# Value rows of the graph layer's first tile made during the mixing's sums, edge counts closed two tiles early, router and shared parts in a new order

## The chip, the core and the metric

The kernel runs on one core of a Trainium2 chip. The core has a matrix engine (TensorE, PE in the profile), a vector engine (VectorE, DVE), a scalar engine (ScalarE, ACT), a general engine (GpSimd, POOL) and a queue engine for transfers (SyncE, SP). Each runs its own list of instructions in order; they wait for each other on semaphores. The metric is the device time of one execution in microseconds.

## The reference

x is 1250 rows of 512. With xn, the layer norm of x, and 40000 edges (src, dst):

```python
Q, K, V = xn @ Wq + bq, xn @ Wk + bk, xn @ Wv + bv        # graph layer: 8 heads of 32
att = exp((Q[receivers] * K[senders]).sum(-1) / sqrt(32)) # one row for each edge
out = relu(segment_sum(att / denom[receivers] * V[senders], receivers))
gnn = xn + relu(relu(out @ Wa + ba) @ Wf + bf)

q, k, v = elu(xn @ mWq.T + bq) + 1, elu(xn @ mWk.T + bk) + 1, xn @ mWv.T + bv   # 8 heads of 64
mix = (q @ (k.T @ v)) / (q @ k.sum() + 1e-6) @ Wo.T + bo

x = x + gnn + mix
h = ln(ln(x))                                             # 64 experts, two for each row
w, idx = top_k(softmax(h @ Wr @ codebook.T / 0.7), 2)
moe = sum over the two experts of w * (silu(h @ W1[e]) @ W2[e] + b2[e])
shared = (silu(h @ Ws1 + bs1) @ Ws2 + bs2) * 0.25
y = moe + shared
x = x + (ln(x) + y + silu(ln(y) @ Wf1 + bf1) @ Wf2 + bf2)
```

## The kernel before

The rows are cut into T = 10 tiles of 125 rows; all matrices are float32. Every engine has one list of instructions written out by hand; their order is the order of work. What is shared between the lists stands in three tables at the head of the file. `TURNS` gives each PSUM result (named `mix_o`, `gnn_v`, `hidden` ...) its bank, in rings: stretches with 6, 4, 6, 2 and 8 banks. Before PE fills a bank it waits (`turn`) until the result that had the bank before was read. `STEPS` says behind which results PE does the next steps of the edge counts. `BESIDE` says which parts of shared work stand beside which pair of expert blocks.

The stages, in order. (1) Norm, transposes of xn, the mixing's queries (`mix_q`), keys and values (`mix_kv`), with the sums k.T v over all tiles in two banks. (2) DVE puts the sums into `kvb` (lines 807 to 815), PE does `rb`, a small product for the router's bias (line 1476), and waits for `kvb_made`. Then come `mix_o` for ten tiles (line 1485; DVE divides, lines 824 to 830), their transposes `moT`, and the output product `mix_wo`. (3) The graph layer's queries and keys, 12 blocks `gnn_qk` (line 1507), which ACT reads (line 1232) and DVE splits in four goes into `qk_hi` and `qk_lo` (lines 846 to 848), stored by POOL to `qk_d`; then the value rows, ten tiles `gnn_v` (line 1513), to which DVE adds the bias (line 856).

Edge counts run beside stages 1 to 3. The 40000 edges are taken in GE = 80 groups. For a group, DVE makes one-hot matrices (lines 749, 751), PE multiplies them into one of two banks (line 1425), and DVE adds the result to `Cx` (line 755) at an offset. One step on DVE is: wait for the group before and add it, then make the one-hots for the group two ahead. PE's step g waits until group g-2 was added. After the last group DVE closes with `cx_made`. PE then transposes `Cx` (line 1530) into `C`, copied by ACT and DVE in turn; SP waits for `cx_made` too, and loads the split queries and keys of the heads (lines 452, 453) into room that the edges' buffers had. (4) Attention with the counts as weights; (5) the two products of the graph layer (`gnn_a`, `gnn_f`), norms, and the rows `yz`, stored to `z_d` for the experts.

(6) The router: logits, the best two of 64, `M1` and `M2` as one-hots and their sum `Mb` (`m_made`). PE sums `Mb`: bank `rank` 0 gives counts for each expert, `rank` 1 and 2 the rank of each row within its expert (line 1660). From the counts DVE makes blocks of 64 rows (`blocks_made`), PE sums these (`base`), DVE compares (`passed_made`), PE gives the blocks' owners (`owner`), after which SP may load experts' weights (`owner_made`). From ranks and base come positions, one-hots `slots` and `rowhot` (`slots_made`), and from them, by PE, the list of rows for each block (`list`), by which POOL gathers rows `Zg`. The combine weights (`wtop`, `prob`, `comb_made`, lines 995 to 1010) are made on DVE between `m_made` and `blocks_made`; PE transposes them (`combT`). Parts of the shared expert fill PE's list in between: `hidden` i (two halves of 8 matmul instructions each, line 1626, read by ACT with silu) and `fb` (line 1692), a fold of the last norm's bias into `bf1`.

(7) The loop over 36 pairs of blocks (and more, if the rows need them). In pair p PE does: the first product (line 1714), the second of pair p-1 (line 1732), the parts in `BESIDE[p]`, two transposes, and the transposes of the gathered rows of pair p+2 (line 1704). The parts are halves of `hidden` 6 to 19 and thirds of `shared` 0 to 7 (line 1640), laid out by the costs in `parts_beside`. POOL gathers (line 601), scatters results (line 606) and in pairs 2 to 11 adds a bias row to XR (line 622), in one list. (8) The experts' rows are read back, normed, and the last two products give the output.

## Time and profile before

| | us |
|---|---|
| median of 3 runs (905.36 to 906.53) | 905.95 |
| the profiled execution | 907.27 |
| its span | 905.5 |
| PE busy in it | 863.5 |
| DVE busy | 522.0 |
| ACT busy | 288.9 |
| POOL busy | 154.0 |

The profile is of one execution. In a timeline a row is a run of equal instructions; the number in brackets is how long the engine was idle before the first, and behind the arrow stands what ended that. Rows named PEld are weight loads that overlap the matmuls. The granted clock is PE's, as a share of 2.4 GHz; 0.50 is 1.2 GHz. In the table of stretches each engine has its busy time and its number of instructions.

### The profile page before, as it was taken

What the parts mean: (1) busy time and instruction counts of PE and PEld (TensorE: products, weight loads), DVE (VectorE), ACT (ScalarE), POOL (GpSimd) and SP (SyncE); (2) the same over time, 40 slices, a digit from 0 to 9 for tenths busy, and PEclk for the clock granted to TensorE, in tenths of its full rate; (3) what the DMA queues carried; (4) which work ended last, traced back from release to release, by engine and by line L of the source; (5) the groups of instructions that cost most, each with busy time, mean ns of one, the idle gap of its engine ahead of it and who ended that gap; (6) DMA issues with size and microseconds to landing.
All of it is one profiled execution on the core that took longest, in us unless ns stands there. A gap on an engine that the chain in (4) does not pass through costs nothing.

```text
span 905.5 us, 11877 instructions
## 1 busy us (share of the span) xinstructions
PE 863.5 (95%) x3978; PEld 492.8 (54%) x3978; DVE 522.0 (58%) x1365; ACT 288.9 (32%) x560; POOL 154.0 (17%) x168
## 2 busy tenths in 40 slices
PE   3999998999998999999999998999999999999898
PEld 2565556745577443344356586546645745654374
DVE  7687777666675899999955484222222223122472
ACT  4531111200104656565434431212222222322273
POOL 6100003200100000000001222234422222222240
PEclk9999998999999999999999998999999999999999
DMA  9410000000418350501022515688989888886722
GB/s 273 158 48 0 1 1 1 1 0 1 167 60 175 76 115 1 114 4 44 11 105 55 179 34 208 252 301 306 318 302 322 312 321 278 325 301 220 182 69 91
DMA packets 41340, 129.81 MB, mean 143 GB/s; under 512 B 8393, under 2 KB 8835, under 8 KB 40639
## 3 DMA queue, kind: packets, MB, share of 16 engines
q1 hardware_dynamic: 32955, 110.76, 37.9%
q0 software_dynamic: 7872, 17.94, 5.4%
q8 instruction: 33, 0.54, 0.2%
q10 hardware_dynamic: 452, 0.34, 0.2%
q14 instruction: 28, 0.23, 0.1%
HBM read 118.48 MB, written 19.68 MB: 153 GB/s over the span
## 4 chain that ended last, share of the span: by engine, by line
PE 67%; DVE 15%; DMA 5%; DVEq 5%; issue 4%; ACT 2%; POOL 1%; SPq 1%; POOLq 0%; ACTq 0%
DVE att L929 8%; PE ps L1464 8%; PE ps L1714 7%; PE ps L1640 7%; PE ps L1732 6%; PE ps L1626 5%; DMA Zg<-z_d,gat 4%; PE ps L1442 4%; PE ps L1498 4%; PE ps L1591 4%; PE ps L1507 4%; PE ps L1425 3%; PE ps L1582 2%; PE ps L1704 2%; PE ps L1783 2%
## 5 line engine op out<-in xcount | busy, mean ns | idle before, releaser
L1073 DVE TENSOR_SCALAR hgT<-ps,cols 128x128 f32<-128x128 f32 x152 | 51.8, 403 | 153.0 <-PE ps L1704 152.9
L929 DVE TENSOR_TENSOR att<-ps,C 125x832 f32<-125x832 f32 (+1 forms) x120 | 119.2, 1005 | 5.6 <-ACT ps L1245 4.9
L1245 ACT ACTIVATE ps<-ps 125x832 f32<-125x832 f32 (+1 forms) x120 | 96.4, 847 | 62.5 <-PE ps L1543 62.5
L1554 PE MATMUL ps<-att,V 125*64 125x416 f32 (+1 forms) x480 | 100.7, 530 | 1.4 <-DVE att L929 1.0
L1626 PE MATMUL ps<-hT,Ws_s 128*128 128x250 f32 x320 | 75.2, 387 | 0.4 <-issue 0.4
L1640 PE MATMUL ps<-Ws_s,hsT 128*125 128x512 f32 x160 | 75.3, 608 | 0.0
L1714 PE MATMUL ps<-W,hgT 128*64 128x256 f32 x576 | 71.6, 392 | 1.0 <-DVE hgT L1073 1.0
L1464 PE MATMUL ps<-mW,xnT 128*125 128x512 f32 x160 | 72.2, 594 | 0.0
L1626 PEld LDWEIGHTS ps<-hT,Ws_s 128*128 128x128 f32 x320 | 60.5, 194 | 20.4 <-issue 13.7
L1732 PE MATMUL ps<-W,ehT 128*64 128x512 f32 x288 | 68.0, 592 | 0.7 <-ACT ehT L1323 0.7
L1543 PE MATMUL ps<-Qst,Kst 128*125 128x416 f32 (+1 forms) x240 | 66.1, 386 | 2.2 <-DVE att L929 1.2
L606 POOL DMA_INDIRECT y_d<-eo,lst x35 | 35.6, 1018 | 181.3 <-ACT eo L1331 181.3
L751 DVE TENSOR_SCALAR ohB<-iotaW,key 125x200 bf16<-125x200 f16 x320 | 64.6, 265 | 0.0
L1543 PEld LDWEIGHTS ps<-Qst,Kst 128*125 128x125 f32 x240 | 37.8, 185 | 47.9 <-issue 30.7
L1331 ACT COPY eo<-ps 128x512 f32<-128x512 f32 x36 | 21.1, 586 | 113.5 <-PE ps L1732 113.5
L1323 ACT ACTIVATE ehT<-ps,b1T 128x64 f32<-128x64 f32 x144 | 33.5, 318 | 69.3 <-PE ps L1722 69.3
L1554 PEld LDWEIGHTS ps<-att,V 125*64 125x64 f32 x480 | 26.5, 135 | 49.9 <-DVE att L929 26.4
L1640 PEld LDWEIGHTS ps<-Ws_s,hsT 128*125 128x125 f32 x160 | 28.0, 187 | 46.3 <-issue 46.3
L1714 PEld LDWEIGHTS ps<-W,hgT 128*64 128x64 f32 x576 | 38.8, 139 | 21.7 <-DVE hgT L1073 1.2
L564 POOL DMA_DIRECT2D z_d<-yz x10 | 5.5, 549 | 249.9 <-DVE yz L964 249.8
L601 POOL DMA_INDIRECT Zg<-z_d,gat x38 | 40.0, 1052 | 39.6 <-DVEq L1090 26.8
L1425 PEld LDWEIGHTS ps<-ohB,ohA 125*128 125x128 bf16 x320 | 30.7, 114 | 27.1 <-issue 24.3
(249 smaller groups left out, 1208.3 us busy)
## 6 DMA issues: line engine op xcount, KB each, us to landing
W<-in_W SPq DMA_DIRECT2D x144, 512.0 KB, 6.3
Kst<-qk_d SPq DMA_DIRECT2D x32, 156.2 KB, 5.4
Qst<-qk_d SPq DMA_DIRECT2D x32, 156.2 KB, 5.6
Yt<-y_d SPq DMA_DIRECT2D x10, 448.0 KB
Ws_s<-in_Ws SPq DMA_DIRECT2D x2, 2048.0 KB, 9.7
qk_d<-qk_hi POOLq DMA_DIRECT2D x4, 625.0 KB, 3.4
qk_d<-qk_lo POOLq DMA_DIRECT2D x4, 625.0 KB, 4.6
z_d<-yz POOLq DMA_DIRECT2D x10, 250.0 KB, 2.7
```

The costliest lines, as they stand in the source:

```text
L751: i = V_.tensor_scalar(ohB[:, s, j, :], iotaW[:, :], key[:, bass.ds(k + j, 1)], None, ALU.is_equal)
L929: V_.tensor_tensor(att[:, n % 3, :, 0:w], scores_of(n, w), C[:, s, o:o + w].unsqueeze(1).to_broadcast([P, 2, w]), ALU.mult).then_inc(att_m ...
L1073: i = V_.tensor_scalar(hgT[:, u, k, :], bank(u, 128, 128, k * 128), col("g1", k), col("b1ln", k), ALU.mult, ALU.add)
L1245: S_.activation(b, b, ACT.Exp, scale=float(DK) ** -0.5).then_inc(s_exp, 1)
L1425: i = MM(bank(b, WN), ohA[:, s, :, j], ohB[:, s, j, :], start=j == 0, stop=j == EG - 1)
L1464: i = MM(bank(b, D, P), xnT[:, k, t * P:t * P + P], mW[:, 1 + w, k, :], start=k == 0, stop=k == KD - 1)
L1543: k = MM(scores_of(n, w)[:, j, :], Kst[:, h % 4, s * P:s * P + P], Qst[:, h % 4, o:o + w], start=True, stop=True)
L1554: k = MM(sums_of(i, 64 * j, 64, w), V[:, s, pair, j:j + 2, :], att[:, n % 3, j, 0:w], start=s == 0, stop=s == T - 1, skip_group_check=True)
L1626: j = MM(bank(b, 250, 128, 250 * half), Ws1_s[:, k, (2 * g + half) * 128:(2 * g + half + 1) * 128], hT[:, k, c * 250:c * 250 + 250], start ...
L1640: i = MM(bank(b, D, P), hsT[:, t // 2 % 2, k, (t % 2) * P:(t % 2) * P + P], Ws2_s[:, k, :], start=False, stop=k == DSH // 128 - 1)
L1714: i = MM(bank(2, DFF, 128, DFF * u)[R * j:R * j + R], hgT[:, u, k, R * j:R * j + R], W1[2 * u + j][:, k, :], start=k == 0, stop=k == KD - ...
L1732: i = MM(bank(4 + u, D)[R * j:R * j + R], ehT[:, u, m, R * j:R * j + R], W2[2 * u + j][:, m, :], start=m == 0, stop=m == 1, skip_group_che ...
```

## The change

1. `gnn_v` of tile 0 is done by PE between `rb` and the wait for `kvb_made` (the wait for the `gW` weights is moved there), and read by DVE right after `rb_s`.
2. `STEPS`: the last `gnn_qk` block gets two count steps, `gnn_v` tiles 1 to 7 one each, tiles 8 and 9 none. DVE closes the counts after tile 7 and reads tiles 8 and 9 behind `cx_made`.
3. Router, DVE: the combine weights are made behind `slots_made`; the second half of the ranks is copied behind `passed_made`. PE: the second half of the ranks stands behind `base`; `hidden` 2 to 5 between `owner` and `list`; `hidden` 6, `combT` and `hidden` 7 behind `list`. ACT reads in this order.
4. `hidden` 6 and 7 leave the loop. `fb` moves from ahead of the loop into it, behind `shared` 3; DVE folds `Wf1_s` there. The table that follows from the costs puts thirds of `shared` 0 and 1 beside pairs 0 (two), 1, 2, 3 and 4, `hidden` 8 from pair 5 on, and both halves of `fb` with half a hidden part beside pair 15. Before, pairs 0 and 1 had `hidden` 6 and 7, and pairs 2 to 6 `shared` 0 and 1.

```diff
@@ -132,7 +132,7 @@
...
-             "mix_wo": [2, 1, 2, 1, 2, 1, 2, 1, 2, 2], "gnn_qk": [1] * 12, "gnn_v": [1, 1, 1, 0, 1, 1, 1, 0, 1, 1]}
+             "mix_wo": [2, 1, 2, 1, 2, 1, 2, 1, 2, 2], "gnn_qk": [1] * 11 + [2], "gnn_v": [0] + [1] * 7 + [0] * 2}
@@ -149,12 +149,12 @@
...
-        if c == 0:
-            parts += [("hidden", i, k) for i in (6, 7) for k in range(2)]
-        else:
+        if c:
             parts += [("hidden", i, k) for i in range(first, first + 4) for k in range(2)]
         parts += [("shared", t, k) for t in (2 * c, 2 * c + 1) for k in range(3)]
-    cost = {"hidden": 4 * 250, "shared": 3 * 512}
+        if c == 1:
+            parts += [("fb", 0, k) for k in range(2)]
+    cost = {"hidden": 4 * 250, "shared": 3 * 512, "fb": 530}
     total, done, table = sum(cost[p[0]] for p in parts), 0, [[] for _ in range(PAIRS0)]
     for part in parts:
         table[min(PAIRS0 - 1, done * PAIRS0 // total)].append(part)
@@ -816,6 +816,13 @@
...
+            def v_kept(t):
+                reads("gnn_v", t)
+                V_.tensor_tensor(V[:, t, :, 0:3:2, :], bank(TURNS.bank("gnn_v", t), HEADS * DK, P).rearrange("p (h j d) -> p h j d", j=2, d=DK),
+                                 row("gbv", HEADS * DK).rearrange("p (h j d) -> p h j d", j=2, d=DK), ALU.add).then_inc(dve_read, 1)
+
+            v_kept(0)
...
-            for t in range(T):
...
+            for t in range(1, 8):
+                v_kept(t)
                 counted_before("gnn_v", t)
...
             v.drain().then_inc(cx_made, 1)
+            for t in (8, 9):
+                v_kept(t)
@@ -991,24 +998,10 @@
...
-            v.wait_ge(gap_exp, 1)
-            V_.tensor_scalar(sm[:, 2, :], sm[:, 1, :], 1.0, None, ALU.add)
...
             V_.tensor_copy(idh[:, :, :], idw[:, :, :])
...
             reads("rank", 0)
@@ -1016,9 +1009,11 @@
...
-            for i in range(2):
+            def ranks(i):
                 reads("rank", 1 + i)
                 V_.tensor_copy(rankS[:, 5 * i:5 * i + 5, :], bank(TURNS.bank("rank", 1 + i), 5 * E, P).rearrange("p (t e) -> p t e", t=5)).then_inc(dve_read, 1)
+
+            ranks(0)
             reads("base", 0)
...
             V_.scalar_tensor_tensor(mine[:, :], iotaB[:, :], starts_s[:, 0:1], passed[:, :], ALU.is_ge, ALU.subtract)
+            v.drain().then_inc(passed_made, 1)
+            ranks(1)
+            v.drain()
             V_.tensor_tensor(rankS[:, :, :], rankS[:, :, :], base_s[:, 0:E].unsqueeze(1).to_broadcast([P, T, E]), ALU.add)
-            v.drain().then_inc(passed_made, 1)
+            v.drain()
...
             v.drain().then_inc(slots_made, 1)
 
+            v.wait_ge(gap_exp, 1)
+            V_.tensor_scalar(sm[:, 2, :], sm[:, 1, :], 1.0, None, ALU.add)
+            v.drain()
+            V_.reciprocal(wtop[:, :, 0:1], sm[:, 2, :].unsqueeze(2))
+            v.drain()
...
+            V_.tensor_scalar(prob[:, :, :], prob[:, :, :], 4.0, None, ALU.mult)
+            v.drain().then_inc(comb_made, 1)
@@ -1088,18 +1102,22 @@
...
+            def fold_last():
+                reads("fb", 0)
+                V_.tensor_tensor(bf1F[:, :], bank(TURNS.bank("fb", 0), 2), col("bf1", 0, 2), ALU.add).then_inc(dve_read, 1)
+                for k in range(KD):
+                    V_.tensor_scalar(Wf1_s[:, k, :], Wf1_s[:, k, :], col("gf", k), None, ALU.mult)
+                v.drain().then_inc(f1_folded, 1)
+
...
+                    if name == "fb" and part == 1:
+                        fold_last()
                 rows_turned(p + 2, p % 2)
@@ -1305,15 +1323,14 @@
...
-            for i in range(4):
+            for i in range(7):
                 shared_hidden(i)
-                if i:
+                if 1 <= i <= 3:
...
-            for i in range(4, 6):
-                shared_hidden(i)
+            shared_hidden(7)
@@ -1475,6 +1492,16 @@
...
+            def graph_v(t):
+                b = turn("gnn_v", t)
+                for k in range(KD):
+                    i = MM(bank(b, HEADS * DK, P), xnT[:, k, t * P:t * P + P], gW[:, 2, k, :], start=k == 0, stop=k == KD - 1)
+                i.then_inc(filled, 1)
+                count_after("gnn_v", t)
+
+            pe.wait_ge(gw_in, 48)
+            graph_v(0)
 
             pe.wait_ge(kvb_made, 1)
             pe.wait_ge(qT_made, 12)
...
+            for t in range(1, T):
+                graph_v(t)
@@ -1652,18 +1674,20 @@
...
+            rank(0)
             pe.wait_ge(blocks_made, 1)
             b = turn("base", 0)
             MM(bank(b, E + 1, P), nblk[:, :], triS[:, :], start=True, stop=True)
             MM(bank(b, 1, E, E + 1), triI[:, :], nblk[:, 0:1], start=True, stop=True).then_inc(filled, 1)
-            whole_hidden(2)
+            rank(1)
...
-            whole_hidden(3)
+            for i in range(2, 6):
+                whole_hidden(i)
+            pe.wait_ge(slots_made, 1)
+            b = turn("list", 0)
+            for n in range(TOPK * T):
+                i = MM(bank(b, 3 * NP), rowhot[:, n, :], slots[:, n, :, :].rearrange("p s q -> p (s q)"), start=n == 0, stop=n == TOPK * T - 1)
+            i.then_inc(filled, 1)
+            whole_hidden(6)
             pe.wait_ge(comb_made, 1)
...
+            whole_hidden(7)
...
+            def last_bias(m):
+                if m == 0:
+                    pe.wait_ge(wf1_in, 16)
+                    turn("fb", 0)
                 for k in range(KD):
-                    i = MM(bank(b, 1, 128, m), Wf1_s[:, k, m:DFF:2], col("bfln", k), start=k == 0, stop=k == KD - 1)
-            i.then_inc(filled, 1)
-            read_by_now("combT", 2)
-            read_by_now("hidden", 5)
-            read_by_now("list", 0)
-            read_by_now("fb", 0)
+                    i = MM(bank(TURNS.bank("fb", 0), 1, 128, m), Wf1_s[:, k, m:DFF:2], col("bfln", k), start=k == 0, stop=k == KD - 1)
+                if m:
+                    i.then_inc(filled, 1)
@@ -1742,6 +1769,8 @@
                 for name, i, part in BESIDE[p]:
                     if name == "hidden":
                         shared_hidden(i, part)
+                    elif name == "fb":
+                        last_bias(part)
                     else:
                         shared_rows(i, part)
```

Not quoted: the order of the banks in `TURNS` follows the new order of work, and the steps from `wtop` to `comb_made` are moved as they are.

## Rows read from the trace of the kernel before

**Rows 1.** The page's first part: busy time, share and instructions of each engine.

```profile
PE 863.5 (95%) x3978; PEld 492.8 (54%) x3978; DVE 522.0 (58%) x1365; ACT 288.9 (32%) x560; POOL 154.0 (17%) x168
```

**Rows 2.** Timeline, wait for `kvb`, quotients: start us, us, engine, line, op, count [idle<-releaser].

```profile
154.01 14.02 PE L1485 MATMUL ps<-kvb,qT 128*125 128x130 f32 x80 [2.44 <-DVEq L815]
...
163.85 0.76 DVE L830 TENSOR_TENSOR mo<-ps,zt 125x256 f32<-125x256 f32 x2
...
168.88 0.76 DVE L830 TENSOR_TENSOR mo<-ps,zt 125x256 f32<-125x256 f32 x2
```

**Rows 3.** Timeline, first value tiles and the count that PE waits for.

```profile
250.99 1.91 PE L1513 MATMUL ps<-gW,xnT 128*125 128x256 f32 x8
...
256.09 0.35 DVE L755 TENSOR_TENSOR Cx<-Cx,ps 128x200 f32 x1
...
256.58 0.51 PE L1425 MATMUL ps<-ohB,ohA 125*128 125x200 bf16 x4 [1.58 <-DVE Cx L755]
...
257.42 0.41 DVE L856 TENSOR_TENSOR V<-ps,rows 125x256 f32<-125x256 f32 x1
```

**Rows 4.** Timeline, end of the counts to the first scores.

```profile
272.61 0.51 PE L1425 MATMUL ps<-ohB,ohA 125*128 125x200 bf16 x4
...
273.70 0.36 DVE L755 TENSOR_TENSOR Cx<-Cx,ps 128x200 f32 x1 [0.20 <-DVE Cx L755]
275.09 0.35 SPq L452 DMA_DIRECT2D Kst<-qk_d  x1
...
275.12 12.85 PE L1530 MATMUL ps<-ident,Cx 128*125 128x128 f32 x100 [2.00 <-DVEq L880]
...
289.37 1.22 PE L1543 MATMUL ps<-Qst,Kst 128*125 128x416 f32 x5 [0.25 <-DMA Qst<-qk_d]
```

**Rows 5.** Table of stretches, PE alone: stretch us, PE busy (count), PEclk, DMA, GB/s.

```profile
255.30:258.70 3.40, 2.12 (x13) 1.00 0.87 353
...
275.80:279.20 3.40, 3.40 (x19) 0.50 0.77 194
279.20:288.00 8.80, 8.77 (x80) 1.00 1.04 221
```

**Rows 6.** Timeline, the router up to the first pair.

```profile
526.91 0.17 DVE L995 TENSOR_SCALAR sm<-sm 125x10 f32<-125x10 f32 x1
...
531.03 0.28 DVE L1013 TENSOR_SCALAR blkI<-ps 64x125 int32<-64x125 f32 x1
...
532.01 0.31 PE L1664 MATMUL ps<-triS,nblk 64*125 64x65 bf16 x1 [1.07 <-DVEq L1018]
...
532.39 5.01 PE L1626 MATMUL ps<-hT,Ws_s 128*128 128x250 f32 x16
...
538.14 0.25 DVE L1041 TENSOR_SCALAR owner<-ps 1x104 int32<-1x104 f32 x1 [1.41 <-PE ps L1672]
...
542.58 3.54 PE L1626 MATMUL ps<-hT,Ws_s 128*128 128x250 f32 x16
...
548.45 2.44 PE L1685 MATMUL ps<-slots,rowhot 125*128 125x156 bf16 x20 [2.32 <-DVEq L1063]
...
554.89 1.93 PE L1692 MATMUL ps<-cols,Wf_s 128*128 128x1 f32 x16
...
559.46 3.44 PE L1714 MATMUL ps<-W,hgT 128*64 128x256 f32 x16 [0.98 <-DVE hgT L1073]
```

**Rows 7.** Timeline of light pairs, and the table of waits from 556 to 842 us.

```profile
599.47 1.05 POOL L601 DMA_INDIRECT Zg<-z_d,gat  x1 [0.16 <-issue]
...
606.70 0.75 PE L1704 MATMUL ps<-ident,Zg 128*128 128x128 f32 x4 [0.88 <-DMA Zg<-z_d,gat]
...
607.38 1.95 PE L1714 MATMUL ps<-W,hgT 128*64 128x256 f32 x16
614.46 1.95 PE L1714 MATMUL ps<-W,hgT 128*64 128x256 f32 x16
...
PE ps L1704 <- DMA Zg<-z_d,gat: 2.6, 6, 0.9
```

64 lines of the change are left out of this document (19 added, 45 removed).

## The prediction, made before the change was timed

> **What bounds the kernel now.** I read the page first: TensorE (PE) is busy for 863.5 of 905.5 us [rows 1], so a gain can come from three things only: its waits, its half clock, and work that is put where it waited. So I went on with the timeline of PE around its long waits, and looked for what the change touches there. The reader should see three places. (a) At 154.01 PE had been idle for 2.44 us, until VectorE (DVE) had built `kvb` [rows 2]. (b) Between the queries' rows and the attention it waits twice: 1.58 us at 256.58 for DVE to add a count [rows 3], and 2.00 us at 275.12 for `cx_made`; the SyncE (SP) loads of heads, which wait for the same semaphore, start at 275.09, and the second score waits at 289.37 for the landing of one of them [rows 4]. (c) In the router it waits 1.07 us for `blocks_made` and 2.32 us for `slots_made` [rows 6]; then comes the pair loop, where PE hardly waits: 2.6 us in six waits, all for a gathered row tile `Zg` [rows 7]. Last the clock: its granted rate falls to 0.50 after the longer waits and comes back to 1.00 some 3.4 us later [rows 5]. After the waits of 2.44, 2.00 and 2.32 us it fell; after that of 1.58 us it did not [rows 3, 5].
>
> All sums are made on the profiled execution, 907.27 us with a span of 905.5; the median of the runs is 905.95, 1.3 less. I take the saving in us from the one and subtract it from the other.
>
> **Part A, value rows of tile 0 before the `kvb` wait.** Eight matmul instructions, 1.74 us of PE (1.91 with the last one's drain [rows 3]), go into the 2.44 us wait; the `gW` weights were loaded long before (the wait for them is moved along, and 110 us lie between). PE does them in time that was lost, and 0.7 us of waiting is left. DVE gets one addition of 0.42 us (as its fellow at 257.42 [rows 3]) between `rb_s` and the first division; the first quotient had to wait for PE anyhow. What is gained in this stage is the clock. With the wait it was half for two stretches (6.8 us), and the ten tiles of `mix_o` took until 169.64 (168.88 plus 0.76 [rows 2]). At full clock DVE sets the pace, 1.258 us a tile ((168.88 - 163.85) / 4 [rows 2]). The first tile would end some 2.0 us after 154.01, at 156.0, and nine more at 167.3: **-2.4 us**. What excludes more: DVE's pace. If the remaining 0.7 us, with the nearly empty one-column matmuls of `rb` ahead of it, still drops the clock, the stage gains nothing and pays up to 0.2 us for the addition. Ends: -2.6 to +0.2. I take -2.4, since a rest of 0.7 us is nearer to the 1.58 us that did no harm.
>
> **Part B, counts closed two tiles early.** In this stretch PE loses tile 0 (1.74 us, done in A). One count step moves ahead, after the last query/key block. For DVE that is one more step (add, one hot A, one hot B: 1.33 us from 256.09 to 257.42 [rows 3]) ahead of the fourth split into `qk_hi` and `qk_lo`; all behind it on DVE is late by some 1.2 us: the split, the two POOL stores of it (which nobody wants before `cx_made`), the router's weights, the fill of `V`, and the first count that PE waits for. PE by contrast gets to that count later only by its own steps: it does block 11, two counts, tile 1, a count, tile 2, and is there at 255.2; the add that lets it on ends at 257.75 instead of 256.5. So the wait of 1.58 us becomes some 2.55 us. From there 7 tiles and 6 counts are left (7 x 1.74 + 6 x 0.345 = 14.25 us) and PE ends at 272.0 instead of 272.96.
> The last count is now two tiles (3.5 us) before that, at 268.5. In the trace 1.39 us pass from the start of the last add to the first load of the heads (273.70 to 275.09 [rows 4]), so `cx_made` comes at about 270.0 and PE, with work until 272.0, no longer waits for it. For its own branch on `levels` I put 0.3 us (0 to 0.9, the time DVE's same branch takes in that 1.39). The 100 transposes then run at full clock: 19 of them went in the 3.4 us at half clock, about 80 in 8.8 us at full [rows 5], so 1.5 us less, 11.35 in place of 12.85. PE is through at 283.65 instead of 287.97 and copies take 0.7. The loads of the heads start 5.05 us earlier, and the one that ended last lands at 284.3. Both releases meet at 284.4 against 289.37 [rows 4]: -4.9 us. The additions for tiles 8 and 9 (2 x 0.42) come on DVE behind `cx_made` and before its first copy of `C`; PE's ring waits for that of tile 8 only with the third transposed block.
> Against it: the longer wait of 2.55 us is of the length after which the clock fell each time. A half-clock stretch inside PE's own chain costs half its 3.4 us, 1.6 to 1.7, and delays the last count too. I take it as happening, since 2.55 is nearer to 2.00-2.44 than to 1.58: **-3.3 us**, ends -4.9 and -1.7 (a second half-clock stretch in the transposes).
>
> A rule of the Trainium skill speaks against the clock's share here. Rows first: PE did nothing but transposes from 279.2 to 288.0 and the granted clock was 1.00 [rows 5]. The Trainium skill, "TensorE: Matmul & The Clock Gate" (Part 4: PE-mode transpose), says that transposes do not count as busy and do not bring the full clock. By that rule a stage of 100 transposes would stay at or fall to half clock, 17.9 us at the pace of 19 in 3.4 us, and part B would lose 1.5 to 6.5 us of its gain. The row disagrees with it, and my sum goes by the row; I give the rule 0.01, inside rival 1.
>
> **Part C, the router.** On DVE the combine weights (526.91 to 531.03, 4.1 us less 0.5 for three id instructions that stay [rows 6]) go behind `slots_made`. On PE the second half of the ranks is done after `base`, hidden parts 2 to 5 stand between `owner` and `list`, 6 and 7 follow, and the bias fold `fb` goes into pair 15 of the loop. Step by step, in the trace's time: `m_made` 526.83; block counts 527.6; first ranks until 528.5 (15 of the 55 matmuls that took 3.4 us); `blocks_made` at 528.6, since DVE is now free, so the 1.07 us wait is nearly gone; `base` until 529.05; 40 ranks until 531.5; DVE has `passed_made` at 530.5; `owner` until 532.25. Four hidden parts at 3.54 to 3.57 us [rows 6], plus 1.4 for a half clock after the ranks as now (5.01 against 3.54 [rows 6]): 547.95. DVE: ranks, sums and the owner block give `owner_made` near 535.7 and `slots_made` at 544.8 (owner row at 534.6; in the trace 10.3 us lie between that row at 538.14 and `list` at 548.45 [rows 6]), 3.1 us ahead of PE, so the 2.32 us wait is gone, and with it the half clock in `list` (2.44 to about 1.4). `list` ends at 549.4, hidden 6 and 7 with the transposed weights (1.23) between them at 557.8; `comb_made` (548.8) is long there. The gathers start 1.5 us earlier than now and land under hidden 6. Transposes 1.2 and the 0.98 us wait for `hgT` [rows 6]: first pair at 560.0, **+0.5 us** against 559.46. But the loop has two hidden parts less (7.14) and `fb` more (1.79 of the 1.93 with drain [rows 6]): **-5.35 us**; and without the waits and one-column matmuls ahead of it the first pair runs at full clock (1.88 in place of 3.44 [rows 6]): **-1.55 us**.
> What can eat this is the gather. It goes out at 599.47, behind that pair's scatter and an addition of POOL, and PE waits for it at 606.70: 7.2 us [rows 7]. A pair with one third of shared rows lasts 7.08 us (607.38 to 614.46 [rows 7]). POOL sends the gather of pair p+3 about 7.1 us after pair p starts (while it still has an addition in each pair) and PE wants it 0.6 us before pair p+2 starts: two pairs must last 7.1 + 7.2 + 0.6 = 14.9 us, two light ones last 14.2. In the new table of parts the light pairs come right at the start: one third each in pairs 1 to 4, then a half hidden part alone (6.15 us) in pairs 6, 9, 16, 19, 26 and 29, against 8, 17 and 26 before. Walking the pairs with these numbers I get waits of 0.8, 0.9 and 0.8 us up to pair 10, and some 4.1 in all against 2.6: **+1.5 us**, ends 0 and +5 (every light pair pays 0.7). Sum of C: 0.5 - 5.35 - 1.55 + 1.5 = **-4.9 us**, ends -6.4 and -1.4. The fold in pair 15, 1.8 us of one-column matmuls, could drop the clock once, 1.7 us; I leave it for the range. DVE's own share of the fold (1.3 us) lies in waits of about 5 us per pair.
>
> **Sum.** -2.4 - 3.3 - 4.9 = -10.6 us: 896.7 for the profiled execution, **895.4** against the median.
>
> **Rivals.**
> 1. *The clock doesn't come back* (the waits that remain drop it all the same). A gives 0, B's transposes stay part slow (-1.8), C loses the 1.0 in `list` and the 1.55 in the first pair (-2.3). For it: where a full wait went, thin matmuls remain (`rb`, ranks, `fb`). Against it: 1.00 after a wait of 1.58 us [rows 5]. Together -4.1: 901.8.
> 2. *The gathers bind the loop.* PE work taken out of the first pairs turns into waiting for `Zg`; C gives only what comes ahead of the loop, about -1. For it: the 14.9 against 14.2 us above. Against it: 2.6 us of such waits in 36 pairs [rows 7], though there were 13 or more light ones. -2.4 - 3.3 - 1 = -6.7: 899.3.
> 3. *Slower.* Late gathers feed on themselves: if a gather in the light pairs needs more than 8.5 us to land (7.2 seen [rows 7]), each of the 20 or so light pairs waits 1 us; if a wait passes 2 us the clock falls too, 1.7 us a time. From +12 us in the loop on (1.5 counted and 10.6), the gain of all else is gone; 20 pairs at 1.0 us, less the 1.5 already counted, make 895.4 + 18.5 = 913.9. Half of the light pairs existed before and did not do so.
> 4. *The stretch isn't early.* If PE's branch on `levels`, or the DVE step ahead of the split, costs as much as the two tiles cover, B gives nothing: -7.3, 898.7.
> 5. *Better than the sum:* no half clock after the 2.55 us wait, no more gather waits than now: -13.7, 892.3.
>
> **Chances.** Forecast, within 2.5 us of 895.4: 0.48. Rival 1: 0.16. Rival 2: 0.12. Rival 4: 0.08. Rival 5: 0.07. Rival 3: 0.05, and 0.04 that several of 1, 2 and 4 come together and leave nothing that can be told from 905.95. A measurement of this kernel tells about 0.2% (1.8 us) from no change. So faster 0.91, same 0.04, slower 0.05. The range 891.5 to 902.0 takes in the forecast and rivals 1, 2, 4 and 5.
>
> **What would show it.** A: PE's wait at `mix_o` 0.7 instead of 2.44 us, and granted clock near 1 there; the ten tiles of quotients done 13.3 instead of 15.6 us after `kvb`. B: an idle time of PE of 2.5 us at the first count behind tile 2, a half-clock stretch after it; none before the transposes; last release of the scores still a head's load or a copy of `C`, within 0.5 us of each other. C: no PE wait before `base` and `list` over 0.3 us, first pair at full clock, waits for `Zg` of 3 to 5 us in all. The prediction is wrong if the `Zg` waits pass 7 us, if the clock is half in `mix_o`, or if the heads' loads, not the transposes, start the attention by more than a microsecond.

## The result, and the profile after

| | before | after |
|---|---|---|
| median, six runs each, same chip | 906.24 (904.48 to 908.81) | 897.24 (896.39 to 898.97) |
| ratio, with its 95% interval | | 0.9904 (0.9887 to 0.9922) |
| the profiled execution, its span | 907.27, 905.5 | 896.39, 894.6 |

The change makes the kernel 8.7 us faster (7.1 to 10.2). The forecast was 895.4, the range 891.5 to 902.0; the measured 897.24 lies 1.8 us above the forecast. Executions of one kernel differ by 2 to 10 us (the 31 runs of the kernel before beside the last experiments went from 903.59 to 910.1), so a profiled execution is one draw from such a spread. What is read off a trace below is set against a median wherever a kernel was run for it.

The page of the kernel after, its first part (busy time, share, instructions of each engine), which answers to [rows 1]:

```profile
PE 858.5 (96%) x3978; PEld 488.3 (55%) x3978; DVE 523.0 (58%) x1365; ACT 288.5 (32%) x560; POOL 153.9 (17%) x168
```

PE is busy for 5 us less (863.5 to 858.5) with the same 3978 instructions, so these 5 us are for the most part clock: the mean granted clock was 0.987 of full speed over 905.5 us and 0.992 over 894.6, which makes, as an estimate, 23.5 us at half clock before and 14.3 after, worth 4.6 us. The span is 10.9 us less, so 5.9 more are waits that went.

**Part A.** Timeline of PE and DVE around the wait for `kvb` (start us, us, engine, line, operation, count, idle time before and its releaser), against [rows 2]:

```profile
151.06 1.99 PE L1499 MATMUL ps<-gW,xnT 128*125 128x256 f32 x8
153.58 9.55 PE L1512 MATMUL ps<-kvb,qT 128*125 128x130 f32 x64 [0.53 <-DVEq L815]
...
153.69 0.41 DVE L821 TENSOR_TENSOR V<-ps,rows 125x256 f32<-125x256 f32 x1
...
166.81 0.75 DVE L837 TENSOR_TENSOR mo<-ps,zt 125x256 f32<-125x256 f32 x2
```

What is left of the wait is 0.53 us, the first value tile (151.06) stands where PE was idle, and from the end of the wait to the end of the last quotient 13.98 us pass (166.81 + 0.75 - 153.58) instead of 15.63. The kernel before had its half clock here from 152.9 us on, for 6.8 us; the kernel after has none.

**Part B.** Timeline from the count that PE waits for to the second score, against [rows 3, 4]:

```profile
255.30 0.35 DVE L755 TENSOR_TENSOR Cx<-Cx,ps 128x200 f32 x1
...
255.80 0.51 PE L1442 MATMUL ps<-ohB,ohA 125*128 125x200 bf16 x4 [2.52 <-DVE Cx L755]
...
268.76 0.35 SPq L452 DMA_DIRECT2D Kst<-qk_d  x1
...
270.10 11.08 PE L1552 MATMUL ps<-ident,Cx 128*125 128x128 f32 x100
...
281.90 0.43 PE L1565 MATMUL ps<-Qst,Kst 128*125 128x416 f32 x1 [0.72 <-DVE C L893]
282.80 1.20 PE L1565 MATMUL ps<-Qst,Kst 128*125 128x416 f32 x5 [0.47 <-DMA Qst<-qk_d]
```

The wait at the count has grown to 2.52 us, as forecast (2.55). The wait ahead of the transposes is gone, the loads of the heads start 6.33 us earlier (275.09 to 268.76) and the second score 6.57 us (289.37 to 282.80). The table of stretches of the kernel after, PE alone (stretch, us and PE busy with count, granted clock, DMA share, GB/s), against [rows 5]:

```profile
252.00:255.80 3.80, 1.28 (x6) 1.00 0.41 163
255.80:259.20 3.40, 3.40 (x21) 1.00 0.47 194
270.10:281.20 11.10, 11.08 (x101) 1.00 1.02 222
285.20:288.60 3.40, 3.35 (x10) 0.50 1.05 220
513.90:517.30 3.40, 3.00 (x9) 0.50 0.28 113
```

No half clock follows the wait of 2.52 us. The transposes run at full clock through 11.1 us. But two half-clock stretches stand where the kernel before had none: behind the first scores, and in the first hidden parts of the router.

**Part C.** Timeline of PE in the router, and of the fold in pair 15, against [rows 6]:

```profile
524.51 0.24 PE L1688 MATMUL ps<-triS,nblk 64*125 64x65 bf16 x1
528.26 15.06 PE L1648 MATMUL ps<-hT,Ws_s 128*128 128x250 f32 x64
543.16 1.53 PE L1703 MATMUL ps<-slots,rowhot 125*128 125x156 bf16 x20
554.49 1.95 PE L1741 MATMUL ps<-W,hgT 128*64 128x256 f32 x16 [0.98 <-DVE hgT L1087]
...
671.88 2.04 PE L1722 MATMUL ps<-cols,Wf_s 128*128 128x1 f32 x16
```

The row for `Zg` (a tile of gathered rows) in the table of waits from 540 to 835 us (total, times, longest), against [rows 7]:

```profile
PE ps L1731 <- DMA Zg<-z_d,gat: 2.8, 4, 0.9
```

`base` and `list` are not waited for, `list` takes 1.53 us in place of 2.44 and the first pair 1.95 in place of 3.44: both at full clock. The waits for `Zg` are what they were.

From mark to mark, in the two profiled executions:

| mark | before | after | gain so far | gain of the step |
|---|---|---|---|---|
| wait for `kvb` ends | 154.01 | 153.58 | 0.43 | 0.43 |
| last quotient starts | 168.88 | 166.81 | 2.07 | 1.64 |
| second score | 289.37 | 282.80 | 6.57 | 4.50 |
| attention over (`gnn_a` starts) | 450.53 | 445.55 | 4.98 | -1.59 |
| first pair | 559.46 | 554.49 | 4.97 | -0.01 |
| last pair | 829.59 | 818.73 | 10.86 | 5.89 |

The first 0.43 us belong to no part: in the profiled kernels that have everything up to this wait as before, it ended anywhere from 152.64 to 154.04 us.

### The profile page after: what moved, and what is told of

It reads as the page before. It is cut to its first block, busy times and chain, and to the rows that moved or that the text cites. A ratio compares the mean times of both kernels' runs of the same rounds, so it can differ in the third digit from the quotient of the medians.

```text
span 894.6 us, 11880 instructions
## 1 busy us (share of the span) xinstructions
PE 858.5 (96%) x3978; PEld 488.3 (55%) x3978; DVE 523.0 (58%) x1365; ACT 288.5 (32%) x560; POOL 153.9 (17%) x168
## 4 chain that ended last, share of the span: by engine, by line
PE 68%; DVE 14%; DMA 5%; issue 4%; DVEq 4%; ACT 2%; POOL 1%; SPq 1%; POOLq 0%; ACTq 0%
DVE att L936 8%; PE ps L1481 8%; PE ps L1662 7%; PE ps L1741 7%; PE ps L1648 6%; PE ps L1759 6%; DMA Zg<-z_d,gat 4%; PE ps L1459 4%; PE ps L1525 4%; PE ps L1613 4%; PE ps L1533 4%; PE ps L1442 3%; PE ps L1604 2%; PE ps L1731 2%; PE ps L1812 2%
## 5 line engine op out<-in xcount | busy, mean ns | idle before, releaser
L755 DVE TENSOR_TENSOR Cx<-Cx,ps 128x200 f32 x80 | 28.5, 356 | 29.9 <-PE ps L1442 17.2
```

## The experiments

Each kernel was timed in five rounds beside the kernel before; a ratio is always to that one, whose median was 905.9 to 906.1 throughout. A difference to the kernel after is one of medians from different rounds; by the ratios the same differences come out up to 0.8 us smaller or larger.

### One part at a time

**A alone.** The first value tile early, the counts' places as before:

```diff
...
-             ... "gnn_qk": [1] * 12, "gnn_v": [1, 1, 1, 0, 1, 1, 1, 0, 1, 1]}
+             ... "gnn_qk": [1] * 12, "gnn_v": [0, 1, 1, 1, 1, 1, 1, 0, 1, 1]}
...
+            pe.wait_ge(gw_in, 48)
+            graph_v(0)
 
             pe.wait_ge(kvb_made, 1)
```

> Only tile 0's value rows are made ahead of the wait for kvb; the counts close after tile 9 as before, the router is as before. Theory: the stage of the quotients gains 1.65 us by the clock (as in the trace after the change, 13.98 instead of 15.63 us), and the stretch of value rows gains the whole tile, 1.74 us, because the wait at its first count keeps its 1.58 us: 3.4 us in all. Rival (the parts add up as their stages did in the changed kernel, where the tile's 1.74 us turned into a longer wait at that count, 2.52 us): 1.65 us only.

Measured 903.67, ratio 0.9976 (0.9957 to 0.9996): -2.2 us, with an interval from 0.4 to 3.9 that takes in the theory and the rival. The trace goes with the theory: the wait at the first count of the value rows is 1.59 us as before, the second score is 3.16 us earlier and the end of the attention 3.11.

**B alone.** All ten value tiles behind the queries and keys; the counts closed two tiles early:

```diff
...
-             ... "gnn_qk": [1] * 12, "gnn_v": [1, 1, 1, 0, 1, 1, 1, 0, 1, 1]}
+             ... "gnn_qk": [1] * 11 + [2], "gnn_v": [0] + [1] * 7 + [0] * 2}
...
             v.drain().then_inc(cx_made, 1)
+            for t in (8, 9):
+                v_kept(t)
```

> Only the counts close two tiles early; tile 0 stays with the other tiles, the router is as before. Theory: the wait at the late count is 0.85 us instead of 2.52, since PE has tile 0 to do in it; the second score starts 4.5 us earlier relative to the first query block, as with both parts, and the half clock either stays away from the transposes and from what follows (4.5 us gained) or falls on the start of the attention (2.9). Rival (the gain needs tile 0 moved away): 2.8 us at the second score.

Measured 902.22, ratio 0.9957 (0.994 to 0.9974): -3.9 us. B is worth something without A. In its trace the wait at the count is 1.13 us (0.85 expected), the second score is 4.18 us earlier, nearer to the theory's 4.5 than to the rival's 2.8, and no half clock stands in the transposes or behind the scores.

**C alone.** The router's new order, hidden 2 to 7 ahead of the loop, and the fold in pair 15; value rows and counts as before. PE's list of it in short:

```diff
-            whole_hidden(2)
+            rank(1)
             pe.wait_ge(passed_made, 1)
...
-            whole_hidden(3)
+            for i in range(2, 6):
+                whole_hidden(i)
+            pe.wait_ge(slots_made, 1)
...
+            whole_hidden(6)
             pe.wait_ge(comb_made, 1)
...
+            whole_hidden(7)
```

> Only the router and the shared parts are in the new order. Theory (PE's work taken out of the loop comes back in full, because the gathers wait no more than before): first pair at the same time or up to 0.5 us later, loop 5.9 us shorter: -5.5 to -6.5 us. Rival (gathers bind): the waits for Zg grow from 2.6 to over 5 us and no more than 3.5 us are gained.

Measured 901.87, ratio 0.9954 (0.9936 to 0.9971): -4.2 us. In its trace `list` starts without a wait, the first pair takes 1.95 us, and the loop from first to last pair is 265.3 us against 270.1. The rival is out: the waits for `Zg` are 2.6 us in seven. The theory's 5.5 to 6.5 us lie at the upper end of the interval (2.6 to 5.8) or above it. One loop is no exact measure either: with the table of parts of the kernel before it took 269.2 to 272.1 us in seven profiled kernels, with that of the kernel after 263.1 to 265.3 in five.

The three make 10.3 us in sum, and together 8.7 (7.1 to 10.2) were measured: within these errors they add up. The forecast's terms (2.4, 3.3, 4.9) each lie inside the interval of their kernel (0.4 to 3.9, 2.4 to 5.4, 2.6 to 5.8), so the medians cannot say which is high and which low; the traces can, below.

### Is A's gain the clock?

The kernel before with only this added, work that nobody uses, so that all it can bring is the clock:

```diff
+            pe.wait_ge(gw_in, 48)
+            b = turn("mix_o", 0)
+            for k in range(KD):
+                MM(bank(b, HEADS * DK, P), xnT[:, k, 0:P], gW[:, 2, k, :], start=k == 0, stop=k == KD - 1)
             pe.wait_ge(kvb_made, 1)
```

> The kernel before, with eight matmul instructions (four products of tile 0 with the value weights, result overwritten) put into PE's wait for kvb as pure extra work; nothing else moves. Theory (part A gains in its stage by the clock alone): no half clock in the quotients, time 1.65 to 2.1 us less although work was added. Rival (the clock falls anyway, or what helps is that work was moved): no change, 0 +- 0.5 us.

Measured 905.66, ratio 1.0 (0.9987 to 1.0014). In the trace of it the mechanism works: the wait is 0.53 us, and the quotients take 13.72 us instead of 15.63, at full clock. Yet nothing is left at the end: the interval (1.2 us faster to 1.3 slower) leaves out the theory's 1.65 to 2.1. The same kernel again:

> The same as e_dummy, a second time, to narrow its interval. The profile of the first showed the quotients 1.9 us shorter and a half-clock stretch at the start of the attention, 2.6 us longer; the times showed no gain. Theory (the clock in the quotients is worth 1.9 us on average, and the stretch in the attention was that execution's): both runs together at least 1 us under before. Rival (the gain is given back on average too): within 0.7 us of before.

Measured 905.52, ratio 0.9995 (0.9978 to 1.0011), so the two together are far from the theory's 1 us or more. The timeline of PE of the first of the two shows where the gain stops, in order of time:

```profile
272.29 11.18 PE L1534 MATMUL ps<-ident,Cx 128*125 128x128 f32 x100 [2.00 <-DVEq L880]
284.19 0.42 PE L1547 MATMUL ps<-Qst,Kst 128*125 128x416 f32 x1 [0.72 <-DVE C L886]
286.33 1.20 PE L1547 MATMUL ps<-Qst,Kst 128*125 128x416 f32 x5 [1.72 <-DMA Qst<-qk_d]
```

and its table of stretches (columns as above) has the clock behind them:

```profile
287.60:291.00 3.40, 2.22 (x6) 0.50 1.02 210
```

Here the wait of 2.00 us ahead of the transposes is not followed by a half clock. They are through in 11.18 us, and then PE waits 1.72 us for the loads; the half clock comes behind that, at the attention's start, and the attention takes 163.8 us in place of 161.2. The second score is 3.0 us earlier than before, the end of the attention 0.4.

This led to a table over the profiled executions, the main finding of the study. The half clock is read from the granted clock in tables of stretches like the one above:

| kernel | first load of the heads | second score | between | half clock in the transposes | half clock behind the scores | second score to `gnn_a` |
|---|---|---|---|---|---|---|
| before | 275.09 | 289.37 | 14.28 | yes | no | 161.2 |
| after | 268.76 | 282.80 | 14.04 | no | yes | 162.8 |
| A alone | 271.83 | 286.21 | 14.38 | yes | no | 161.2 |
| B alone | 270.79 | 285.19 | 14.40 | no | no | 161.2 |
| C alone | 272.76 | 286.95 | 14.19 | yes | yes | 162.8 |
| unused products | 272.26 | 286.33 | 14.07 | no | yes | 163.8 |
| unused products, again | 272.66 | 286.87 | 14.21 | no | yes | 163.9 |

(The seven profiled kernels that follow lie between 14.10 and 14.41 too, and have 161.2, 162.7 to 162.8, or 163.9 to 164.0 us.) Two things follow. First, the second score comes 14.0 to 14.4 us after the first load of the heads, whether the transposes took 11.1 us or 12.9: a half clock inside them costs nothing there, and what moves the attention's start is `cx_made` alone. The chain of the kernel after shows what the 14 us are: SP issues a load every 0.46 us, the sixteenth (the last of the first two heads) at 275.82, and that one takes 6.93 us to land.

Second, a half clock behind the scores costs about 1.6 us where it lasts 3.4 us (162.8 against 161.2) and 2.7 where it lasts 6.8. Whether it comes is only in part a matter of the wait for the loads. In all four profiled kernels where PE waited longest there (1.72 to 1.86 us: the unused products twice, and two kernels below that start from the kernel before) it came; in the ten with a wait of 0.17 to 0.84 us it came in five, and B alone waited 0.83 and had none where the kernel after waited 0.47 and had one. So transposes at full clock behind a wait of 2.00 us have not brought anything: PE is through earlier, waits longer for the loads, and the half clock stands behind the scores.

In the two profiles the gain of the unused products was lost to it. The other executions say the same on average. Each has its mean granted clock on record, and 2 x (1 - clock) x span is an estimate of its time at half clock. The 22 and 26 executions of the kernel before beside these had 22.2 and 22.3 us of it on average, the 24 with the unused products 20.9. The products take up to 6.8 us of half clock out of the quotients, but only some 1.4 us of it are gone from the whole: the rest came back elsewhere. What makes it come back is not shown.

### What holds the counts' end

The wait of 2.52 us says that DVE's list binds there. Two pieces of it have no hurry: the kernel after with

```diff
                     counted_before("gnn_qk", 3 * i + c)
+                    if (i, c) == (0, 2):
+                        for k in range(KD):
+                            w = V_.tensor_scalar(Wr_s[:, k, :], Wr_s[:, k, :], col("g1", k), None, ALU.mult)
+                        w.then_inc(wr_scaled, 1)
+                    if (i, c) == (1, 1):
+                        V_.memset(V[:, :, :, 1, :], 1.0)
...
-            for k in range(KD):
-                i = V_.tensor_scalar(Wr_s[:, k, :], Wr_s[:, k, :], col("g1", k), None, ALU.mult)
-            i.then_inc(wr_scaled, 1)
-            V_.memset(V[:, :, :, 1, :], 1.0)
             for t in range(1, 8):
```

> The changed kernel, with DVE's scaling of the router's weights and its fill of V done earlier, in its waits beside the query/key blocks, so that they no longer stand ahead of the count that PE waits for. Theory (the wait of 2.52 us at that count is DVE's list, and it holds the last count, the transposes and the heads' loads): wait about 0.5 us, second score 2 us earlier, 2 us less than the changed kernel, some 11 less than before. Rival (the heads' loads or the clock hold the start of the attention): the wait shrinks but under 0.5 us is gained.

Measured 894.80, ratio 0.9869 (0.9846 to 0.9892): 2.4 us less than the kernel after, and the lowest median of all; its interval just touches that of the kernel after. PE's timeline in the trace of it:

```profile
254.43 0.51 PE L1444 MATMUL ps<-ohB,ohA 125*128 125x200 bf16 x4 [1.09 <-DVE Cx L755]
...
268.73 11.08 PE L1554 MATMUL ps<-ident,Cx 128*125 128x128 f32 x100
280.52 0.43 PE L1567 MATMUL ps<-Qst,Kst 128*125 128x416 f32 x1 [0.72 <-DVE C L895]
281.49 1.21 PE L1567 MATMUL ps<-Qst,Kst 128*125 128x416 f32 x5 [0.53 <-DMA Qst<-qk_d]
...
442.70 4.58 PE L1606 MATMUL ps<-aggT,Wa_s 128*128 128x500 f32 x10
```

The wait fell by 1.43 us and the second score came 1.31 earlier (2 us were expected of both). In this execution the rest of what it is ahead at the attention's end (2.85 us) is the half clock behind the scores, which it does not have (161.2 us to `gnn_a`).

The same two pieces moved in the kernel before, without and with the unused products, ask whether both gains come through when DVE is not late. First without:

> The kernel before, with two pieces of DVE's list moved: the scaling of `Wr_s` behind the third query/key block and the fill of `V` behind the fifth, instead of both behind the last split and ahead of the first value tile. Nothing of the change is in it. Theory (the first count that PE waits for is DVE's, and all that follows up to the attention's start hangs on it): the wait of 1.58 us at that count falls to about 0.2, and the last count, the loads of the heads and the second score all come 1.4 us earlier, about 14.1 us from the first load to the second score as in every kernel so far; median 904.5. Rival (the start of the attention is held by something else, and these DVE steps have cover): the wait is gone, the second score where it was, 905.9.

Measured 905.05, ratio 0.9982 (0.9966 to 0.9999): about -1.6 by the ratio. The median lies halfway between the theory's 904.5 and the rival's 905.9; the trace goes with the theory. The wait at the count fell to 0.25 us, and the wait for `cx_made` stayed 2.00, since from the last count to `cx_made` the chain is fixed. The profiled execution is the slowest of its twelve (909.66): second score 1.5 us earlier, then a half clock at 289.5 and 163.9 us to `gnn_a`, so its end says nothing of the median.

The same with the products added:

> The kernel before with the same two DVE pieces moved, and the four useless products in PE's wait for `kvb` added. It asks whether the 1.9 us that the products win in the quotients, and that were lost again by the attention's start in two profiled runs, come through once DVE's list isn't the bound behind them. Theory (they were lost to DVE's list and to the half clock after the wait that it makes): PE comes to the first awaited count 1.9 us earlier and finds most of it done, so 1.0 to 1.9 us less than the kernel with the moved pieces alone: 902.6 to 903.5. Rival (whatever is won ahead of the attention there falls to a half clock at its start): as the kernel with the moved pieces alone, 904.5, with its half-clock stretch within 5 us of the second score and 162.8 us or more from the second score to the end of the attention instead of 161.2.

Measured 904.43, ratio 0.9977 (0.9955 to 0.9999), from 900.9 to 908.8 in twelve runs. That is 0.6 us less than the kernel without the products, not to be told from nothing, and outside the theory's 902.6 to 903.5 (the means of the twelve, 904.24 and 905.21, are 1.0 apart). The rival's signs are there in the profiled execution: a half clock 2.2 us behind the second score, 162.7 us to `gnn_a`. So the 1.9 us from the clock in the quotients did not reach the end in any of three kernels by more than their scatter. A alone did, by 2.2 us: it also takes 1.74 us of work out of the stretch behind the queries and keys, and that part is no clock effect. With intervals of 2 us each way, A alone and the unused products are not clearly apart, though.

### What holds the loop

POOL's ten additions to XR stand between scatters and gathers in pairs 2 to 11. To see whether they hold the gathers, the kernel after with all ten ahead of the first gather:

```diff
+            for t in range(T):
+                gp.wait_ge(xy_kept, t + 1)
+                nc.gpsimd.tensor_tensor(XR[:, t, :], XR[:, t, :], row("bf2"), ALU.add).then_inc(bf2_added, 1)
             gp.wait_ge(gat_made, 1)
...
-                if 2 <= p < 2 + T:
-                    t = p - 2
-                    gp.wait_ge(xy_kept, T)
-                    nc.gpsimd.tensor_tensor(XR[:, t, :], XR[:, t, :], row("bf2"), ALU.add).then_inc(bf2_added, 1)
```

> The changed kernel, with POOL's ten bias additions to XR done while it waits for the list, not between the gathers of pairs 2 to 11. Theory (in these pairs the gather is late because it goes out behind an addition of 1.3 us): no wait of PE for Zg in pairs 2 to 11, 1.5 to 2.5 us less than the changed kernel. Rival: the additions slow DVE's chain to slots_made (13 us of POOL work beside it), which has 2 us to spare, or the waits come back later in the loop: under 0.5 us gained, or lost.

Measured 902.73, ratio 0.9957 (0.9941 to 0.9973): 5.5 us slower than the kernel after. The theory is out: the loop did not get shorter (264.4 against 264.2 us, 2.4 us of `Zg` waits in six). The loss stands ahead of it, mostly in the router: in the profiled executions the attention ends 1.3 us later than in the kernel after, `list` starts 5.9 and the first pair 6.1 us later. DVE and POOL there, and PE's first product that waits, in this kernel:

```profile
524.16 1.10 DVE L1003 CAST idh<-idw 125x40 bf16<-125x40 int32 x1
525.18 0.27 DVE L1005 TENSOR_SCALAR blkI<-ps 64x125 int32<-64x125 f32 x1
525.18 7.39 POOL L612 TENSOR_TENSOR XR<-XR,rows 125x512 f32<-125x512 f32 x6
525.54 0.98 DVE L1007 TENSOR_SCALAR blkI<-blkI 64x125 int32<-64x125 int32 x1
526.60 1.14 DVE L1009 TENSOR_SCALAR nblk<-blkI 64x125 bf16<-64x125 int32 x1
527.82 0.31 PE L1687 MATMUL ps<-triS,nblk 64*125 64x65 bf16 x1 [2.87 <-DVEq L1010]
```

and in the kernel after:

```profile
522.63 0.18 DVE L1004 CAST idh<-idw 125x40 bf16<-125x40 int32 x1
523.53 0.28 DVE L1006 TENSOR_SCALAR blkI<-ps 64x125 int32<-64x125 f32 x1 [0.72 <-PE ps L1675]
523.91 0.22 DVE L1008 TENSOR_SCALAR blkI<-blkI 64x125 int32<-64x125 int32 x1
524.20 0.22 DVE L1010 TENSOR_SCALAR nblk<-blkI 64x125 bf16<-64x125 int32 x1
```

Three DVE instructions of 0.2 us take 1.0 to 1.1 us while POOL does additions of 1.23 us each (7.39 / 6), one behind the other; the one that reads PSUM (`blkI<-ps`) keeps its 0.27. An addition starts at 525.18, so the next ones start at about 526.41 and 527.64, and the three instructions end at 525.26, 526.52 and 527.74, each about 0.1 us behind the end of an addition. The Trainium skill, "SBUF — State Buffer" (SBUF: two separate sides), says that DVE and GpSimd share a pair of ports, held for a whole instruction by a GpSimd instruction or by a DVE instruction of certain forms, so that the loser waits for the other to end. The trace agrees with that rule by these ends, and no DVE instruction in this stretch grew by more than one addition of POOL.

PE waits 2.87 us for the blocks, and that is not all of the loss: behind the wait the granted clock is 0.50 from 528 to 536 us, and from `base` to hidden 2 PE takes 6.01 us (527.82 to 533.83) where the kernel after takes 3.75.

Both moves at once, the early DVE pieces and the additions:

> Both of these at once. Theory: they add, 3.5 to 4.5 us less than the changed kernel, about 893 us. Rival: what either gains is taken back by the other or by a half-clock stretch: no more than 2 us.

Measured 898.05, ratio 0.9912 (0.9893 to 0.9931), 3.3 us more than with the DVE pieces alone, and not the 893 of the theory: the early DVE pieces are a gain with and without the additions moved, the moved additions are a loss both times.

**Hidden 6 and 7 in the loop again**, the router's new order kept. Is the shorter loop just work that was moved to the other side?

```diff
     ("list", ["dve"]),
-    ("hidden", ["act"]),
     ("combT", ["act"] * 3),
...
-        if c:
+        if c == 0:
+            parts += [("hidden", i, k) for i in (6, 7) for k in range(2)]
+        else:
...
-            whole_hidden(6)
             pe.wait_ge(comb_made, 1)
...
-            whole_hidden(7)
```

> The kernel after with its new order of the router, but hidden parts 6 and 7 beside pairs 0 and 1 again (PE goes from `list` by the transposed weights straight to the first row transposes). It asks what the 5.9 us are that the loop got shorter by. Rival (work is work: the parts may stand on either side): the first pair 7.1 us earlier, the loop 7.1 us longer, 897.2, or up to 1 us less as the first gathers have more time to each pair. Theory (hidden 6 and 7 cover the way from `list` to the first gathered rows: DVE's index steps, POOL's gathers and their landing): PE waits 4 to 6 us for `Zg` ahead of the first pair, the clock falls after it (1.6), the loop is 7.1 longer: 902 to 904.

Measured 904.72, ratio 0.9981 (0.9964 to 0.9999): 7.5 us slower than the kernel after. PE's timeline:

```profile
546.37 1.72 PE L1709 MATMUL ps<-ident,prob 125*64 125x125 f32 x10 [2.02 <-DVEq L1077]
552.00 2.22 PE L1729 MATMUL ps<-ident,Zg 128*128 128x128 f32 x8 [3.91 <-DMA Zg<-z_d,gat]
554.56 1.97 PE L1739 MATMUL ps<-W,hgT 128*64 128x256 f32 x8 [0.34 <-DVE hgT L1088]
```

The first pair starts 11.74 us after `list`, against 11.33 in the kernel after, though 7.1 us of work are gone from between: PE waits 2.02 us for the combine weights and 3.91 for the first gathered rows, and goes on at half clock (2.22 us for the transposes that take 1.11, 3.26 for the first pair). The loop is 271.4 us, 7.2 longer. So in these two executions the two parts are free ahead of the loop and cost their full 7.2 us in it.

**The fold ahead of the loop again**, the rest as after: `fb` between the transposed weights and hidden 7, with DVE's part of it ahead of the first pair:

```diff
+            pe.wait_ge(wf1_in, 16)
+            b = turn("fb", 0)
+            for m in range(2):
+                for k in range(KD):
+                    i = MM(bank(b, 1, 128, m), Wf1_s[:, k, m:DFF:2], col("bfln", k), start=k == 0, stop=k == KD - 1)
+            i.then_inc(filled, 1)
             whole_hidden(7)
...
-        if c == 1:
-            parts += [("fb", 0, k) for k in range(2)]
```

> The kernel after, with the fold `fb` ahead of the loop again (one-column matmuls between the transposed weights and hidden 7; DVE adds and scales ahead of the loop). Theory (the fold is PE work of 1.8 us wherever it stands, and neither place has a wait that it could fill): 0 difference, 897.2, unless the one-column matmuls cost the clock as in the kernel before, where the first pair then ran at half: +1.6, 898.8, with the first pair at 3.4 us instead of 1.95. Rival (its place in pair 15 hides it in the waits for `Zg`, or it lengthens a chain of DVE ahead of the first pair): 899.0 or more at full clock, the first pair's wait for `hgT` longer than 0.98 us.

Measured 900.58, ratio 0.9939 (0.9916 to 0.9961): 3.3 us more than the kernel after: the rival's number (899.0 or more at full clock), and the theory's 0 or 1.6 (with a half clock) are out. One of the rival's two reasons is out as well. The first pair ran at full clock with its wait of 0.98 us as always, 13.22 us behind `list` instead of 11.33: 1.9 us for the fold. (Hidden 7 stands between the fold and the first pair here. In the seven profiled kernels with the router's old order the fold stands right ahead of the rows' transposes, and the first pair took 3.26 to 3.68 us in all of them.) But the loop, with 1.9 us less to do, took 265.9 us instead of 264.2. The waits for `Zg` from 557 to 835 us in this kernel:

```profile
PE ps L1739 <- DMA Zg<-z_d,gat: 6.4, 6, 1.9
```

They are 6.4 us against 2.8. Without the fold the parts stand in other pairs: pairs 1 to 5 and 30 to 35 have a single part each, in place of 1 to 4 and 31 to 35, and the longest wait (1.86 us, at 601.44) stands behind the first of these runs. That looks like the mechanism of the forecast's second rival; it is worth 3.6 us here, in one profiled execution, and no run tests the reading by itself.

## Why the prediction was right, point by point

**Part A** (forecast -2.4). The mechanism came as forecast: the work in the wait, a rest of 0.53 us that does not drop the clock, DVE's pace. The term was mis-sized: -1.64 in the trace. The first quotients ended 2.46 us after the wait instead of 2.0 (155.28 + 0.76 in the trace of after), PE stopped once for 0.44 us (at 163.57, for a quotient), and a tile took 1.28 us. More weighty is what the sum did not ask: whether a gain at 166 us reaches 905. The unused products won 1.9 us there and nothing in the median. What A brought alone (-2.2, 3.2 at the second score in its trace) fits the 1.74 us that it takes out of the next stretch as well as it fits the clock, and the sum had put that 1.74 under B.

**Part B** (forecast -3.3, trace -4.5). Right were the wait at the count (2.55 forecast, 2.52 seen), the 100 transposes at full clock (11.35 forecast, 11.08 seen), and that PE no longer waits for `cx_made`. The step that failed is the half clock after the wait of 2.55 us, counted at 1.6 because its length is near to those after which the clock fell. It did not come (1.00 from 252.0 to 259.2). Nor did it in the three later kernels with the same wait of 2.52 us. A wait's length alone does not decide this: of the seven waits of 2.00 us at the transposes, three (before, A alone, C alone) were followed by a half clock there and four (the unused products twice, and the two kernels before with moved DVE pieces) were not; and behind a wait of 2.33 us `list` took 1.54 us, at full clock, in A alone and B alone, where it took 2.44 behind 2.32 us in the kernel before. The prediction also weighed a rule of the Trainium skill, that transposes bring no full clock ("TensorE: Matmul & The Clock Gate", Part 4: PE-mode transpose). The trace disagrees with it again: 1.00 through 11.1 us of nothing else. A second step was idle: the 1.5 us that the transposes save at full clock are not on the path, since the loads take 14.0 to 14.4 us from the first issue on. The forecast had both releases meet and did not see that the loads decide in every kernel, here by 0.47 us (under the microsecond that it named as a sign of being wrong).

**The attention** (forecast 0, trace +1.6) **and the first hidden parts** (forecast 0, trace +1.4: 8.38 us where two parts took 6.99). Both are half-clock stretches in new places, in the spirit of rival 1, but not where it looked for them: what stands ahead of them (a wait of 1.25 us for DVE behind the second score, the small products and waits of 0.4 to 0.55 us ahead of hidden 0) stands there in the kernel before too, with no half clock behind it. The sum gave these two stages no clock term at all. B's and C's surplus and these two cancel, and so the total came out close (10.6 forecast, 10.9 in the trace, 8.7 by the ratio). That is partly luck.

**Part C** (forecast -4.9). The waits before `base` and `list` went, both at full clock, and the first pair took 1.95 us. Up to the start of the first pair the forecast had +0.5; the trace has 0.0 (a gain of 4.97 us there, 4.98 at the end of the attention), although 1.4 us of new half clock are in it, so this term was too dear by 1.9 us. The loop: by the trace's rows, 7.1 us less by the two hidden parts, 2.0 more by the fold, 1.5 less in the first pair at full clock makes -6.6; PE's busy time fell by 6.4 and its idle time rose by 0.5 (2.6 to 3.1): -5.9, against -5.4 with the 1.5 us for gathers. This term was too high: the waits for `Zg` went from 2.6 to 2.8 us. The walk through the pairs took each light pair's gather at the 7.2 us of the one seen; in the kernel before they took 3.2 to 8.3 us from issue to landing, 6.5 in the middle. It wasn't baseless, as the fold's place shows (6.4 us with another table). In the medians, C alone gave 4.2.

**The rivals.** 1 (the clock does not come back): in part, by 3.0 us in two places that it did not name. 2 (gathers bind the loop): not in this kernel. 3 (slower by late gathers): no sign. 4 (the stretch isn't early): no, the heads' loads start 6.33 us earlier, and B alone gave 3.9. 5 (no half clock after the 2.55 us wait, no more gather waits): both of its conditions held, and without the two new half clocks the median would have been about 894.2 (897.24 less 3.0, an estimate), 1.9 us above its 892.3.

## What to carry to other kernels

Before a gain is counted, ask which release starts the next stage, and measure it from that release: here the heads' loads set the attention's start 14 us after one semaphore, and what made PE faster in between brought nothing. Work moved out of a saturated loop is worth its full length only where it lands in a wait; hidden 6 and 7 ahead of the first gathered rows were such a case, and the same parts inside cost 7.2 us. On an engine whose clock falls after waits, a saved wait is not a saved microsecond until several executions say so: the half clock that it removes can come back in another stage.

## What the runs showed of the hardware

- The same half clock comes at different places in executions that differ little: behind a wait of 2.00 us it came in three profiled kernels and not in four; after 2.52 us it did not come in any of four. It costs 1.6 to 2.8 us on the path and nothing where loads are the longer way (12.85 against 11.08 us of transposes, the same 14.0 to 14.4 us to the second score).
- Executions of one kernel scatter by 2 to 10 us. A part of it is this clock: over the 31 executions of the kernel before, the estimated time at half clock (14 to 31 us) and the device time go together with a correlation of 0.66.
- 100 fp32 transposes of 128 x 128 back to back ran with the clock granted at 1.00, 11.08 us.
- Three DVE instructions of 0.2 us beside POOL's additions took 1.0 to 1.1 us, each until just behind the end of an addition of 1.23 us; one that read PSUM kept its 0.27 us.
